# Key rows of every visit's second pair gathered by GpSimd, and a row buffer of ten pairs, in a graph attention kernel

## What is computed

```python
h = relu(layernorm(x))
# layer 0: attention over edges (8 heads of 32), then feed-forward
q, k, v = split(layernorm(h) @ Wqkv + bqkv)
scores = einsum("ehd,ehd->eh", q[src] * SCALE, k[dst])
e = exp(scores - segment_max(scores, dst)[dst])
agg = segment_sum(v[src] * (e / segment_sum(e, dst)[dst]), dst)
y = h + agg
x = x + y + gelu(layernorm(y) @ W_in + b_in) @ W_out + b_out
# layer 1: relational convolution, 8 relations from 4 bases
h = relu(layernorm(x))
W = einsum("rb,bio->rio", comp, basis)
h_all = einsum("ni,rio->nro", h, W)
agg = segment_sum(h_all[src, edge_type], dst)
z = gelu(agg + h @ loop_w + h_bias + h)
x = x + layernorm(z) * gamma + beta
```

## Time and profile before

| | us |
|---|---|
| median of 3 runs | 1527.08 |
| lowest, highest | 1525.3, 1531.56 |
| the profiled execution | 1523.96 |
| its span | 1522.1 |
| TensorE, matmuls busy | 1138.3 (75%) |
| VectorE busy | 898.6 (59%) |
| GpSimd busy | 918.3 (60%) |
| ScalarE busy | 448.1 (29%) |

### The profile page before, as it was taken

One profiled execution on the slowest core, in us unless ns is written; L12 is line 12 of the kernel. 1 busy time (PEld: TensorE's weight loads), 2 busy tenths in 40 slices (PEclk: granted clock), 3 DMA queues, 4 the chain that ended last, 5 costly groups with the idle time before them and its releaser, 6 DMA issues.

```text
span 1522.1 us, 18355 instructions
## 1 busy us (share of the span) xinstructions
PE 1138.3 (75%) x5319; PEld 846.0 (56%) x5319; DVE 898.6 (59%) x2826; ACT 448.1 (29%) x1150; POOL 918.3 (60%) x983
## 2 busy tenths in 40 slices
PE   5784879999999999999999993554645555554543
PEld 2442667777787777777777652333534334443432
DVE  5762678878887887887888630133425443442425
ACT  4652224454454444445445330000000000000000
POOL 3855666666666666666666004666666666766651
PEclk9997899999999999999999996767767876776766
DMA  7768776777877777777676212333433343343431
GB/s 243 215 188 264 214 223 210 248 238 231 272 228 239 250 237 237 229 245 220 228 252 223 78 58 72 105 110 113 123 114 112 113 116 115 115 121 108 119 95 56
DMA packets 142977, 265.55 MB, mean 174 GB/s; under 512 B 41594, under 2 KB 89828, under 8 KB 139930
## 3 DMA queue, kind: packets, MB, share of 16 engines
q0 software_dynamic: 52480, 160.68, 35.3%
q1 hardware_dynamic: 89434, 102.48, 20.7%
q10 hardware_dynamic: 960, 1.18, 0.2%
HBM read 199.25 MB, written 65.01 MB: 174 GB/s over the span
## 4 chain that ended last, share of the span: by engine, by line
DVE 31%; issue 20%; another core or an unknown queue 18%; PE 18%; ACT 5%; DMA 0%; DVEq 0%; POOL 0%; POOLq 0%; ACTq 0%
DVE arena L1807 5%; DVE arena L1812 5%; PE ps L1539 5%; DVE arena L1742 4%; PE ps L1506 3%; PE ps L1679 3%; DVE arena L1860 2%; PE ps L1565 2%; PE ps L1495 2%; DVE arena L689 2%; ACT arena L1314 1%; ACT L1298 1%; DVE arena L692 1%; DVE arena L671 1%
## 5 line engine op out<-in xcount | busy, mean ns | idle before, releaser
L1222 POOL DMA_INDIRECT arena<-qv_tab,srcs x392 | 383.3, 978 | 229.4 <-PE ps L1506 127.4
L1265 POOL DMA_INDIRECT arena<-h_all,typs x392 | 376.1, 959 | 236.2 <-issue 112.9
L1679 PE MATMUL ps<-arena 128*128 128x256 f32 x784 | 248.1, 477 | 92.2 <-DMA arena<-h_all,typs 47.5
L1679 PEld LDWEIGHTS ps<-arena 128*128 128x128 f32 x784 | 184.5, 243 | 150.5 <-issue 52.1
L1506 PE MATMUL ps<-arena 128*128 128x264 f32 x784 | 213.7, 401 | 35.3 <-DVE arena L1742 24.4
L1565 PE MATMUL ps<-wrel,arena 128*128 128x512 f32 x400 | 188.0, 595 | 2.3 <-ACT arena L1330 2.3
L1506 PEld LDWEIGHTS ps<-arena 128*128 128x128 f32 x784 | 139.3, 193 | 73.8 <-DVE arena L1742 32.0
L1742 DVE TENSOR_TENSOR arena<-arena 128x512 f32<-128x512 f32 x196 | 143.8, 734 | 40.7 <-ACT arena L1298 33.4
L1495 PE MATMUL ps<-arena 128*128 128x264 bf16 x1032 | 143.4, 280 | 12.4 <-DMA arena<-k_tab 12.2
L1495 PEld LDWEIGHTS ps<-arena 128*128 128x128 bf16 x1032 | 125.6, 145 | 46.6 <-issue 37.2
L1807 DVE TENSOR_TENSOR arena<-arena,ps 128x512 f32<-128x512 f32 x172 | 117.4, 683 | 49.1 <-remote 24.0
(11 more groups left out here) (166 smaller groups left out, 1488.1 us busy)
## 6 DMA issues: line engine op xcount, KB each, us to landing
h_all<-arena SPq DMA_DIRECT2D x23, 1024.0 KB
arena<-dst SPq DMA_DIRECT2D x49, 256.0 KB
...
```

The lines of the kernel that those rows point to most:

```text
L1222: pool.indirect_dma_start(out=rowbuf[:, u * T + t, 0:2 * D], out_offset=None, in_=qv_tab, in_offset=bass.IndirectOffsetOnAxis(ap=srcs[:, v ...
L1265: pool.indirect_dma_start(out=rows1[:, u * T + t, :], out_offset=None, in_=h_all[0:N * R, :], in_offset=bass.IndirectOffsetOnAxis(ap=typs[ ...
L1679: last = nc.tensor.matmul(ps[:, 6 + u, 0:D], ind1[:, u, t, :], rows1[:, u * T + t, :], start=(t == 0), stop=(v == 0 and t == T - 1))
```

## The change

The row buffer was two halves of four pairs, one for even and one for odd visits. It becomes a ring of ten pairs: pair j of visit v lies at place (4v + j) mod 10, and GpSimd waits for the pair ten before in place of eight before. Each place has its own semaphore, whose count a formula gives (`ring_count`, and `ring_total` for the third stage, which now goes on with eight of these semaphores in place of its own).

`gathered(v, j)` is now true for pair 1 of every visit, not of odd visits alone. So TensorE no longer makes the key rows of pair 1 in the 25 even visits, and GpSimd gathers them. The tile `kg` becomes two, one for even and one for odd visits, each with its semaphore. The key gathers now follow tile 5 in place of tile 3, and `residual` follows tile 7 in place of tile 3. The arena grows from 25600 to 26240 words for each partition. All else, TensorE's, ScalarE's and VectorE's lists among it, keeps its order.

```diff
--- before.py
+++ after.py
@@ -36,7 +36,7 @@
 WIN = 128
 NWIN = -(-N // WIN)
 LASTW = (NWIN - 1) * WIN
-AWORDS = 25600
+AWORDS = 26240
 KW = D + H
 AW = D + H
 RP = 5
@@ -698,9 +698,20 @@
         GENERAL, IS_WIDE, SPECIAL = 0, 1, 2
 
 
+        RING = 10
+
+        def ring(v, j):
+            return (PAIRS * v + j) % RING
+
+        def ring_count(v, j):
+            return 32 * ((PAIRS * v + j) // RING + 1)
+
+        def ring_total(q):
+            return 32 * len(range(q, G * PAIRS, RING))
+
         with nc.Block() as block:
             cut = carve()
-            rowbuf = cut([2 * T, 2 * D + H])
+            rowbuf = cut([2 * RING, 2 * D + H])
             ind = cut([2, T, WIN])
             indT = cut([2, GE], BF16)
             car = cut([2, WIN])
@@ -713,12 +724,12 @@
             h1T = cut([2, 2, P])
             h1s = cut([2, D])
             zero = cut([D])
-            kg = cut([2, KW])
+            kg = cut([2, 2, KW])
             rec = cut([H])
             stp, mvp, vp, tp, rp = cut([6]), cut([2, 2]), cut([2, 1]), cut([2, 1]), cut([2, 1])
             stf, mvf, vf, tf, rf, nf = cut([6]), cut([2]), cut([1]), cut([1]), cut([2, 1]), cut([2, 1])
-            k_ready, k_used, kg_in = sem("key_rows_ready"), sem("scores_ready"), sem("keys_gathered")
-            row_in = [sem(f"rows_in{j}") for j in range(2 * PAIRS)]
+            k_ready, k_used, kg_in = sem("key_rows_ready"), sem("scores_ready"), [sem(f"keys_gathered{u}") for u in range(2)]
+            row_in = [sem(f"rows_in{j}") for j in range(RING)]
             indT_ready, car_ready = sem("indT_ready"), sem("car_ready")
             turn_ready, ind_ready = sem("turn_ready"), sem("ind_ready")
             exp_done, w_ready, agg_done = sem("exp_done"), sem("weighted_ready"), sem("summed")
@@ -766,7 +777,7 @@
             LASTM = hid_of(LASTV)
 
             def gathered(v, j):
-                return v % 2 == 1 and j == 1
+                return j == 1
 
             def keys_before(v):
                 return sum(not gathered(a, j) for a in range(v) for j in range(PAIRS))
@@ -1003,7 +1014,6 @@
             dl = cut([2, T])
             car1 = cut([2, WIN])
             osum1 = cut([2, D])
-            row1_in = [sem(f"messages_in{j}") for j in range(2 * PAIRS)]
             dl_ready, ind1_ready, car1_ready, agg1_done = sem("dl_ready"), sem("ind1_ready"), sem("car1_ready"), sem("summed1")
             win1_done, osum1_ready, rel_out = sem("window1_done"), sem("osum1_ready"), sem("rel_out")
             h1c_ready, h1t_psum, h1T1_ready = sem("h1_copied"), sem("h1_turned1"), sem("h1T1_ready")
@@ -1217,15 +1227,16 @@
                 def gather(v):
                     u = v % 2
                     for t in range(T):
-                        if t % 2 == 0 and v >= 2:
-                            pool.wait_ge(agg_done, PAIRS * (v - 2) + t // 2 + 1)
+                        q = ring(v, t // 2)
+                        if t % 2 == 0 and PAIRS * v + t // 2 >= RING:
+                            pool.wait_ge(agg_done, PAIRS * v + t // 2 - RING + 1)
                         pool.indirect_dma_start(
-                            out=rowbuf[:, u * T + t, 0:2 * D], out_offset=None, in_=qv_tab,
+                            out=rowbuf[:, 2 * q + t % 2, 0:2 * D], out_offset=None, in_=qv_tab,
                             in_offset=bass.IndirectOffsetOnAxis(ap=srcs[:, v * T + t:v * T + t + 1], axis=0)
-                        ).then_inc(row_in[u * PAIRS + t // 2], 16)
-                        if t % 2 and gathered(v, t // 2):
-                            gather_keys(v, t // 2)
-                        if t == 3 and v >= 1 and out_of(v - 1) is not None:
+                        ).then_inc(row_in[q], 16)
+                        if t == 5 and gathered(v, 1):
+                            gather_keys(v, 1)
+                        if t == 7 and v >= 1 and out_of(v - 1) is not None:
                             residual(out_of(v - 1))
 
                 def gather_keys(v, j):
@@ -1233,9 +1244,9 @@
                         pool.wait_ge(k_used, PAIRS * (v - 2) + j + 1)
                     for t in (2 * j, 2 * j + 1):
                         pool.indirect_dma_start(
-                            out=kg[:, t % 2, :], out_offset=None, in_=kf_tab,
+                            out=kg[:, v % 2, t % 2, :], out_offset=None, in_=kf_tab,
                             in_offset=bass.IndirectOffsetOnAxis(ap=dsti[:, v * T + t:v * T + t + 1], axis=0)
-                        ).then_inc(kg_in, 16)
+                        ).then_inc(kg_in[v % 2], 16)
 
                 def residual(m):
                     if m == 0:
@@ -1265,7 +1276,7 @@
                         pool.indirect_dma_start(
                             out=rows1[:, u * T + t, :], out_offset=None, in_=h_all[0:N * R, :],
                             in_offset=bass.IndirectOffsetOnAxis(ap=typs[:, v * T + t:v * T + t + 1], axis=0)
-                        ).then_inc(row1_in[u * PAIRS + t // 2], 16)
+                        ).then_inc(row_in[u * PAIRS + t // 2], 16)
 
             @block.scalar
             def _(act):
@@ -1293,7 +1304,7 @@
                                              ACT.Copy).then_inc(ind_ready, 1)
 
                 def weights(v, j):
-                    at = v % 2 * T + 2 * j
+                    at = 2 * ring(v, j)
                     act.wait_ge(k_used, PAIRS * v + j + 1)
                     nc.scalar.activation(rowbuf[:, at:at + 2, 2 * D:2 * D + H], sco[:, 2 * j:2 * j + 2, :], ACT.Exp,
                                          bias=nbias[:, :], scale=SCALE).then_inc(exp_done, 1)
@@ -1503,7 +1514,7 @@
                     if j == 0 and v >= 1:
                         pe.wait_ge(osum_ready, v)
                     for t in (2 * j, 2 * j + 1):
-                        last = nc.tensor.matmul(ps[:, AGG, 0:AW], ind[:, v % 2, t, :], rowbuf[:, v % 2 * T + t, D:2 * D + H],
+                        last = nc.tensor.matmul(ps[:, AGG, 0:AW], ind[:, v % 2, t, :], rowbuf[:, 2 * ring(v, j) + t % 2, D:2 * D + H],
                                                 start=(t == 0), stop=(v == 0 and t == T - 1))
                     last.then_inc(agg_done, 1)
 
@@ -1675,7 +1686,7 @@
                         pe.wait_ge(osum1_ready, v - 1)
                     for t in range(T):
                         if t % 2 == 0:
-                            pe.wait_ge(row1_in[u * PAIRS + t // 2], 32 * (v // 2) + 32)
+                            pe.wait_ge(row_in[u * PAIRS + t // 2], ring_total(u * PAIRS + t // 2) + 32 * (v // 2) + 32)
                         last = nc.tensor.matmul(ps[:, 6 + u, 0:D], ind1[:, u, t, :], rows1[:, u * T + t, :],
                                                 start=(t == 0), stop=(v == 0 and t == T - 1))
                         if t % 2:
@@ -1725,7 +1736,7 @@
 
                 def key_rows(v, j):
                     bank = 2 * (j % 2)
-                    return kg if gathered(v, j) else ps[:, bank:bank + 2, 0:KW]
+                    return kg[:, v % 2, :, :] if gathered(v, j) else ps[:, bank:bank + 2, 0:KW]
 
                 def shift(v, j, reduced):
 
@@ -1798,10 +1809,10 @@
                     hid, out = hid_of(v), out_of(v)
                     u = v % 2
                     for j in range(PAIRS):
-                        b = rowbuf[:, u * T + 2 * j:u * T + 2 * j + 2, :]
-                        dve.wait_ge(row_in[u * PAIRS + j], 32 * (v // 2) + 32)
+                        b = rowbuf[:, 2 * ring(v, j):2 * ring(v, j) + 2, :]
+                        dve.wait_ge(row_in[ring(v, j)], ring_count(v, j))
                         if gathered(v, j):
-                            dve.wait_ge(kg_in, 32 * (v // 2) + 32)
+                            dve.wait_ge(kg_in[v % 2], 32 * (v // 2) + 32)
                         else:
                             dve.wait_ge(k_ready, keys_upto(v, j))
                         own.did(nc.vector.tensor_tensor(b[:, :, 0:D], b[:, :, 0:D], key_rows(v, j)[:, :, 0:D], ALU.mult))
```

## The result

The changed kernel takes 1604.23 us in the median of 4 runs (1595.8 to 1608.76) against 1526.76 us of the kernel before on the same chip: ratio 1.0495, 95% interval 1.0445 to 1.0546. It is 5% slower; 1520.5 was forecast, and 1533 was the range's upper end. The profiled execution took 1595.8 us.

The account below looks back on a forecast made before the run. Each pair of visits was taken as bound by VectorE's leg (11.88 us), then TensorE's (17.47 us). First visits -2.5 and residual shift -2.5 took 1524.0 to 1519; 1520.5 was the middle between 1519 and 1522; range 1507 to 1533.

Parts of the forecast that it names:

- (a): Pair 1 of even visits: six matmuls, 0.67 us, leave TensorE but hide behind VectorE's leg in the steady stretch; worth 0.
- Rival one: TensorE is the bound after all, so its removed 16.8 us come off the time: 1507 us; chance 0.2.
- (b): First visits, 131 to 240 us: VectorE waits for TensorE, so removing the keys shortens the chain, together about 2.5 us.
- (c): Visit 0, pair 1: VectorE waits for gathered keys until 139 to 140 in place of 135.26; a later wait hides it.
- (e): Ring of ten for eight: earlier rows worth 0 in the steady stretch, as VectorE does not wait for rows there.
- (g): DMA: 0.27 MB more per pair of visits, 9 GB/s on 240; nothing on the path waits for a transfer: 0.
- (d): GpSimd's queue: two more gathers per even visit, 27.6 of 29.35 us filled; worth 0 while it stays under 29.35.
- Rival three: GpSimd becomes the bound once a gather slot is above 1.36 us; at 1.40, 1542 us; chance 0.07.
- (f): GpSimd's residual adds move later, clear of VectorE's weighting (L1742), which they stretch; worth 2.5 us, ends 0 and 10.
- Rival two: VectorE and GpSimd contend for the SBUF port at the multiply of pair 1 of even visits: 11 us, 1535; chance 0.1.

Follow-up runs that it names:

- d_no_gather: Changed kernel without the two added key gathers of even visits, except in visit 0; those key rows are left out, TensorE's six matmuls stay away: ratio 1.0054.
- a_ring_only: Changed kernel with TensorE making the key rows of pair 1 of even visits again; the ring of ten and the later places stay: ratio 1.0039.
- b_ring8: Changed kernel with a ring of eight pairs instead of ten, key rows of pair 1 still gathered in every visit: ratio 1.0641.
- s_bunch16_pause: Changed kernel, no key gathers after visits 0 and 1, one ring wait per visit, spare GpSimd additions after a visit's second, fourth, sixth gather: ratio 1.0123.
- f_sp_load: Changed kernel with SP loading two blocks of key rows in order instead of the added gathers after visit 0; wrong key rows there: ratio 1.0044.
- h_small: Changed kernel whose two added gathers of even visits after visit 0 fetch 132 bytes per row, not 1056; most key values left out: ratio 1.0547.

## Why the prediction was wrong

- **(a) TensorE's six matmuls worth 0: right.** d_no_gather and a_ring_only differ by 0.15%. TensorE's idle before `add_up` of pair 1 is 0.98 us in the rows above for the 0.83 forecast. Rival one, the bound TensorE, falls with it. TensorE's total busy time did not go down by 17 us as forecast but up by 14.5: the 150 matmuls of L1506 are gone, yet `hidden` alone is busy 13.2 us more (L1550, 111.9 us for 98.7), part of it at 1.2 GHz.
- **(b) The first visits 2.5 us shorter: wrong in sign, and misread.** The prediction puts VectorE's 12.10 us before 149.85 down to the relation products. But TensorE has made these keys at 143.38, by its record, and then sits idle itself, while GpSimd issues 18 gathers in a row until 149.82. The kernel before, TensorE and GpSimd:

```profile
142.54 0.84 PE L1495 MATMUL ps<-arena 128*128 128x264 bf16 x6
151.91 2.13 PE L1506 MATMUL ps<-arena 128*128 128x264 f32 x4 [6.97 <-DVE arena L1742]
148.88 0.95 POOL L1222 DMA_INDIRECT arena<-qv_tab,srcs  x1 [0.30 <-issue]
```

The same after, TensorE and VectorE, in a train of 24 gathers:

```profile
145.08 0.84 PE L1506 MATMUL ps<-arena 128*128 128x264 bf16 x6
156.24 0.69 DVE L1818 TENSOR_TENSOR arena<-arena,ps 128x512 f32<-128x512 f32 x1 [11.98 <-remote]
```

So the effect that the prediction lacks stood in its own rows: the result is 6.5 us late before and 10.3 us late after. The first `statistics` comes 20.1 us later. a_ring_only and d_no_gather have it at 239.1 and 240.0 us, so it isn't the added gathers alone; the larger ring lets GpSimd start with longer trains. b_ring8, the changed kernel with the old size of ring, has it at 236.0 for 245.0; s_bunch16_pause, with the ring and with pauses, at 221.4, ahead of the kernel before. These are single executions, and they agree with the density; a run for this part was not made.
- **(c) Keys of visit 0: right.** VectorE waits 3.05 us for them and multiplies at 141.76, 11.7 us after GpSimd's first gather for the 12 to 13 forecast, and its next wait hides it.
- **(e) The ring and (g) the bytes, worth 0: right for (g)** by f_sp_load. The ring and the later places together cost 0.4% at 18 gathers (a_ring_only); at 20 the ring is worth about 1.5% (b_ring8).
- **(d) is the step that failed: two gathers more on GpSimd's queue, "Worth 0, while the queue stays under 29.35."** The sum of the slots was right (1.25 to 1.3 us each, GpSimd still has waits), rows do land in time, and the queue is not the bound. Rival three had the right engine and the wrong mechanism (GpSimd still waits for TensorE), and its 1542 was too small. What the step lacks is an effect of gathers on another engine: at 18 gathers and 29.35 us the slack of 4.4 us lay as pauses between pairs of gathers; the two added ones used 2.5 us of it, and what went were the pauses (trains of up to 6 gathers became trains of up to 9). Four and more gathers within 5 us then fell more often where ScalarE and VectorE wait for TensorE: VectorE's wait before the multiply with TensorE's keys grew from 11.3 to 54.2 us between 300 and 880 us, and TensorE's before `turn_y` from 0.8 to 27.6. The pairs of visits in which TensorE's clock was at 1.2 GHz for a stretch, after idle time of up to 2.7 us, took 2.3 us more, every second or third pair.
- **(f) The collision of the adds with the weighting goes: right, 743 to 683 ns, and worth nothing to be seen.** a_ring_only has the adds at the later place too; its weighting takes 717 ns, and it is at 1.004.
- **Rival two, the port: right in kind, small.** The multiplies with gathered keys take 834 ns for 682, 6 us in all, and in d_no_gather 687 ns. By the Trainium skill (SBUF — State Buffer, Who interferes with whom) that was the part to fear; the trace agrees in kind, and it is a tenth of the loss.

Beside the measurements stands one page, which no run here tests: the Trainium skill (DMA: Bandwidth & Descriptors, SWDGE vs HWDGE vs iDMA) says that GpSimd writes the descriptors of its transfers to rings kept in SBUF, and that transfers issued by SP don't take this path. f_sp_load and h_small agree with it in so far as the path and not the bytes decide. Where TensorE's results are held, in its work, in PSUM or in the signal, stays open.

No version here beats the kernel before; a_ring_only, d_no_gather and f_sp_load come within 0.6% of it, and two of these leave work out.
